# The second half of a key stack read behind the shift rows

## The reference

```python
x = x + tanh(g_xattn) * xattn(layernorm(x), ctx)
x = x + tanh(g_ffn)   * ffn(layernorm(x))

def xattn(x, xa):                 # 16 heads of width 8
    q, k, v    = split_heads(x  @ Wqkv     + bqkv)
    qa, ka, va = split_heads(xa @ Wqkv_aux + bqkv_aux)
    p  = softmax(q @ k.T  / sqrt(8))      # the token's own keys
    pa = softmax(q @ ka.T / sqrt(8))      # the context's keys
    return (p @ v * (1 - gate) + pa @ va * gate) @ Wo + bo

def ffn(x):                       # 64 experts of width 64, 8 chosen per token, one shared
    w = top-8 weights within the 4 best of 8 groups of sigmoid(x @ gate_w.T)
    return sum_e w[:, e] * (silu(x @ Wg[e]) * (x @ Wu[e])) @ Wd[e] + shared(x)
```

## Time and profile before

| | |
|---|---|
| three runs | 865.65, 865.96, 867.04 us; median 865.96 |
| profiled execution | 866.37 us, span 864.3 us |
| mean granted TensorE clock | 0.986 of full speed |
| busy: TensorE (matmuls) | 832.1 us, 96% of the span |
| TensorE (weight loads) | 647.3 us, 75% |
| DVE | 692.8 us, 80% |
| POOL | 635.6 us, 74% |
| ACT | 570.1 us, 66% |
| SP's and ACT's DMA queue | 57.6% and 0.5% of 16 DMA engines' span |
| chain that ended last | PE 85%, DVE 5%, DMA 3%, issue 3%, ACT 2% |

### The profile page before, as it was taken

The page is one execution under the profiler, slowest core; times in us unless marked ns, Lnnn a source line. Parts: engine busy times, 40 slices in busy tenths (PEclk is TensorE's granted clock), DMA queues, the critical chain, the costliest instruction groups (busy, mean ns, idle before and its releaser), DMA issues.

```text
span 864.3 us, 20204 instructions
## 1 busy us (share of the span) xinstructions
PE 832.1 (96%) x6733; PEld 647.3 (75%) x6733; DVE 692.8 (80%) x1656; ACT 570.1 (66%) x964; POOL 635.6 (74%) x602
## 2 busy tenths in 40 slices
PE   4899999999999889999999999999999999999997
PEld 2467777777766678888888888878888888888885
DVE  6788888888888769769788887867886977886655
ACT  4378888888877766575566666558557556656554
POOL 2567888888864368777886887677787788788785
PEclk9599999999999999999999999999999999999999
DMA  4668777787663156556555654754755655655552
GB/s 118 164 157 175 168 180 162 165 183 156 157 144 68 39 144 155 131 132 148 134 128 143 151 130 114 166 140 103 167 129 133 150 141 124 150 124 151 135 135 61
DMA packets 108035, 120.02 MB, mean 139 GB/s; under 512 B 28560, under 2 KB 70352, under 8 KB 106496
## 3 DMA queue, kind: packets, MB, share of 16 engines
q1 hardware_dynamic: 105056, 118.23, 57.6%
q10 hardware_dynamic: 2880, 0.59, 0.5%
HBM read 103.55 MB, written 14.71 MB: 137 GB/s over the span
## 4 chain that ended last, share of the span: by engine, by line
PE 85%; DVE 5%; DMA 3%; issue 3%; ACT 2%; POOL 0%; SPq 0%; DVEq 0%; ACTq 0%; POOLq 0%
PE bank L1957 20%; PE bank L1958 20%; PE bank L1959 20%; PE bank L1302 6%; PE bank L1289 4%; PE bank L1276 4%; PE bank L1258 2%; DMA stack_q<-nmaxT 2%; PE bank L1246 1%; DVE mx L981 1%; PE bank L1323 1%; DMA cwb<-wts_scratch 1%; PE bank L1252 1%; PE bank L1310 1%; PE bank L1934 1%
## 5 line engine op out<-in xcount | busy, mean ns | idle before, releaser
L1634 POOL TENSOR_TENSOR hid<-act,cwb 128x512 f32<-128x512 f32 x264 | 422.3, 1611 | 128.1 <-DVE act L1861 62.2
L1687 ACT ACTIVATE silu<-bank 128x512 f32<-128x512 f32 x256 | 152.8, 597 | 182.2 <-PE bank L1959 176.9
L1861 DVE TENSOR_TENSOR act<-silu,bank 128x512 f32<-128x512 f32 (+1 forms) x264 | 180.2, 683 | 110.4 <-ACT silu L1687 75.7
L1869 DVE TENSOR_TENSOR hlo<-hid,hhi 128x512 fp32r<-128x512 f32 x256 | 206.8, 808 | 9.9 <-ACT hhi L1693 9.6
L1957 PE MATMUL bank<-xhi,weights_hi 128*128 128x512 f32 x520 | 206.6, 397 | 0.9 <-ACT silu L1687 0.9
L1959 PE MATMUL bank<-xlo,weights_hi 128*128 128x512 f32 x520 | 204.1, 393 | 0.0
L1958 PE MATMUL bank<-xhi,weights_lo 128*128 128x512 f32 x520 | 204.0, 392 | 0.0
L981 DVE TENSOR_REDUCE mx<-bank 128x4 f32<-128x512 f32 x256 | 166.3, 682 | 22.5 <-PE bank L1276 22.1
L1693 ACT ACTIVATE hhi<-hid 128x512 fp32r<-128x512 f32 (+1 forms) x264 | 164.9, 625 | 23.3 <-POOL hid L1634 20.7
L783 ACT ACTIVATE prob<-bank 128x1024 f32<-128x1024 f32 x128 | 131.2, 1025 | 52.0 <-PE bank L1289 48.6
L1957 PEld LDWEIGHTS bank<-xhi,weights_hi 128*128 128x128 f32 x520 | 97.6, 188 | 22.5 <-ACT silu L1687 1.5
(11 more groups left out here) (235 smaller groups left out, 1001.0 us busy)
## 6 DMA issues: line engine op xcount, KB each, us to landing
cwb<-wts_scratch SPq DMA_DIRECT2D x174, 384.0 KB, 5.4
stack_k<-k_scratch SPq DMA_DIRECT2D x30, 256.0 KB, 4.7
k_scratch<-parts_k SPq DMA_DIRECT2D x15, 384.0 KB, 3.2
stack_q<-q_scratch SPq DMA_DIRECT2D x30, 128.0 KB, 2.9
stack_k<-k_scratch SPq DMA_DIRECT2D x30, 128.0 KB, 5.4
q_scratch<-parts_q SPq DMA_DIRECT2D x15, 192.0 KB, 2.2
xin<-in_x_dram SPq DMA_DIRECT2D x16, 128.0 KB, 2.6
cin<-in_ctx_dram SPq DMA_DIRECT2D x16, 128.0 KB, 2.8
```

Of the source, the lines that this page charges most:

```text
L1634: pool.tensor_tensor(h_buf[k][:], a_buf[k][:], cwb[slot][:, q % GP, :], ALU.mult).then_inc(h_ok, 1)
L1687: act.activation(s_buf[k % RS][:], g_bank[k % 2][:], ACT.Silu).then_inc(s_ok, 1)
L1861: nc.vector.tensor_tensor(a_buf[k % RS][at], s_buf[k % RS][at], u_bank[k % 3][at], ALU.mult).then_inc(a_ok, 1)
L1869: nc.vector.tensor_tensor(hlo[k % RH][:], h_buf[k % RS][:], hhi[k % RH][:].bitcast(F32), ALU.subtract).then_inc(hl_ok, 1)
```

## The change

In every chunk that still has a stack to read (n = 0 to 13), the two DMAs of the key stack's half 1 are issued where they stood; then SyncE waits until the shift rows of batch 2n + 2 have landed, and only then issues the two DMAs of half 0. All that stood behind them, `store_x2(n - 1)` first, stands behind the wait too.

```diff
--- before.py
+++ after.py
@@ -425,12 +425,12 @@
                 load_products(stack_q[s][PARTS_AT[half]:PARTS_AT[half] + ROWS_S].rearrange("p h c t -> p (h c t)"),
                               q_v[n], False, half, HH * TC, stk[half][s])
 
-        def load_stack_k(n):
+        def load_stack_k(n, halves=(1, 0)):
 
             s = n % NST
             wait(sp, st_mm, UNITS * CH * (n - NST + 1))
             wait(sp, k_st[n % 2], 16 * ((n + 1) // 2))
-            for half in (1, 0):
+            for half in halves:
                 load_products(stack_k[s][PARTS_AT[half]:PARTS_AT[half] + ROWS_S].rearrange("p h c a t -> p (h c a t)"),
                               k_v[n], True, half, 2 * HH * TC, stk[half][s])
 
@@ -522,7 +522,9 @@
                 if g < LOOPS - 2:
                     expert_weights(g, j)
                 if not last:
-                    load_stack_k(n + 2)
+                    load_stack_k(n + 2, (1,))
+                    wait(sp, shift, 16 * (CH * n + 3))
+                    load_stack_k(n + 2, (0,))
                 if n > 0:
                     store_x2(n - 1, 1 - j)
                 if last and j == 0:
```

## The result

Over 22 executions of each kernel, the changed kernel's median is 868.57 us (865.40 to 872.97) against 866.00 us (864.29 to 868.55). The ratio is 1.0031, with a 95% interval of 1.0019 to 1.0042: slower by 0.3%, 2.6 us. The fastest executions of the two lie 1.1 us apart, but 7 of the changed kernel's 22 are above 870 us and none of the other's is. So the change adds a loss of varying size. The forecast was 865.2 us and no difference.

What follows compares the result with a forecast made beforehand. In attention, matmuls were taken as the bound, with visible loss only in two shift-row stalls. Terms -0.89 + 0.1 = -0.8 us took the 865.96 us median to 865.2, no difference that can be told; 8-in-10 range 864.3 to 868.0.

Steps and rivals of the forecast that it cites:

- The gain: Attention stage: shift rows land in 4.4 us against a budget of 6.3, so TensorE's two stalls go: -0.89 us.
- rival A: Shift rows wait for what is ahead, not the second half; stalls stay, 866.0 up to 867.8 us; chance 0.20.
- The term for the second half: Fifth unit's scores: delayed second half lands at 9.5 us against a 10.4 us budget; 0.1 us put in for edge pairs.
- Rival B: Second half becomes the bound at the even batch's fifth-unit scores, 14 chunks: 869 to 873 us; chance 0.14.
- (4): SyncE's work queued behind the new wait (reads, residual's store, q store) is covered by its wait for POOL: cost 0.
- SyncE's wait of 46.5 us: SyncE's 13 waits for POOL's q split over the attention stage, the cover for the hold, would fall under 15 us.
- All pairs take 16.0 us: Attention stage: with shift rows gone from TensorE's waits, every pair of batches takes 16.0 us.

Runs made afterwards that it cites:

- experiment 9: The changed kernel run once more, unaltered, on the chip of three other runs: 867.13 us, ratio 1.0017 to the kernel before; its profiled execution took 874.32 us.
- Experiment 2: Changed kernel, but all four key reads go out as before the change and only then SyncE waits for the shift rows: 865.99 us, ratio 1.0007.
- Experiment 5: Changed kernel with the hold ended by ACT's third exponential of the odd batch, about 4.0 us after the shift rows' issue, instead of their landing: 865.60 us, 0.9993.
- experiments 10 and 11: Changed kernel with SyncE's hold ended by POOL's q split, 4.47 or 5.16 us after the shift rows' issue: 865.71 us (1.0003) and 870.72 us (1.0075).
- experiment 3: Changed kernel without SyncE's new wait; ACT issues the second half's reads after its third exponential in the odd batch: 867.07 us, ratio 1.0018.
- experiment 12: Changed kernel with q reads behind the key store and the hold ended by ACT's third exponential instead of the rows' landing: 869.48 us, 1.0047.
- experiments 6 and 8: Changed kernel with the hold ended by ACT's fourth exponential: 881.46 us (1.0173); changed kernel with q reads issued behind the key store: 870.31 us (1.0041).
- experiment 13: Changed kernel with the two expert-weight reads moved behind the first half and ahead of the wait for the shift rows: 875.58 us, ratio 1.0118.

## Why the prediction was wrong

**The gain was right.** The rows' landing without the second half beside it was taken as 4.4 us (3.9 to 4.9); it measured 4.0 on average, and both stalls of the earlier trace rows went. That speaks against rival A's outcome: with the second half out of the way the longest landing in the changed profile was 5.4 us, not 6.9, though experiment 9 has one of 6.45 and a wait of 0.4 us behind it. Of rival A's mechanism more is left. Experiment 2, with both halves beside the rows, has a mean of 5.1 us, so holding one of them took off 1.1 us and four fifths stayed. By the rule of the Trainium skill, DMA: Bandwidth & Descriptors, section Queues, rings and completion order, that the prediction set against it (turns between queues, packet by packet), most of the landing should have stayed, and on the mean it did. The longest fell from 6.7 to 5.4 us in the first trace, and that was enough for the stalls. What else is under way counts too: in the chunk of stack 14, with no expert weights read and the first half issued 0.8 us behind s, the rows had landed at 2.1 us.

**The term for the second half was right, at its middle.** Its landing stayed inside the budget of 10.4 us: no 48-row load waited for it in either trace of the changed kernel. Rival B was the right sign for a wrong reason. It named L1276 waiting for the key stack, and that row did come, but for the other half.

**The step that failed is (4), "Cost: 0."** It went as far as the next thing on SyncE, and three of its numbers were short:

- "SyncE is through at s + 4.4 + 1.2 + 0.45 = 166.2, 0.15 us past it" used the mean of the landing. The place was right (the q store went out at s + 6.3 on the mean), but the landing ranged from 2.1 to 5.4 us, to 6.45 in experiment 9. What SyncE has to do by s + 5.92 lets a hold be 4.2 us at most without delay; 5 of 14 holds were 4.6 or more. A long issue (1.6 us) among those behind the hold has the same effect, and no longer falls into a wait.
- It left out the landing of the q store itself. The two held reads, 384 KB, and the store of x2 are now issued just ahead of it, and it takes 3.5 us instead of 2.2. (With the store of x2 alone ahead of it, in experiment 2, it took 2.5.) The 1.3 us more was in no sum, though the same text counted with reads holding up a transfer on ACT's queue.
- "The next first half might go out 0.5 us late, and it has about 2 us" is the step that turned. In the chunk shown above it went out 2.8 us later, nearly all of it by the delays of the q store (1.15 us) and of the reads of q behind it (1.65). The wait of the key store for POOL (9.0 us), which was to take a delay up, fell to 2.1 us in one chunk, and was soon used up. The slack was about right; 2.8 passes it. Its working was not: 167.09 is a load that had already stalled for 0.64 us, and without that 1.35 us is left. The traces give it better: first halves issued up to s + 0.8 were in time in the changed kernel's trace and those from s + 1.05 on were late, and before the change the one in the table of issues above went out 0.8 us ahead of its s. That makes 1.6 to 1.9 us.

Experiment 5 shows that the second point alone fits in the slack, experiments 10 and 11 where the slack ends, and experiment 9 that the late first halves are nearly the whole loss of a bad execution. In experiment 2 the block alone cost nothing that can be told. Experiment 5 differs from the changed kernel only in what ends the hold, at the same mean. What turns a mean that is free (4.0) into 0.3% is then the spread, the holds past about 4.5 us and the long issues behind a hold; that this is so in the executions without a trace is concluded from the curve and two traces, not seen in each.

"SyncE's wait of 46.5 us … falls under 15 us" held (5.6). The wait for the rows was 31.9 us instead of 60, since SyncE itself came later to the wait. "All pairs take 16.0 us" failed in four.

**Open.** The price of late reads without a block (experiment 3, 0.18%) may be the same loop by way of the q store (2.6 us) or ACT's part. How the loss in an execution divides between more stalls and the half-clock stretch behind the longer ones isn't known beyond the two shown. No version was measurably faster than the kernel before: the best (0.9993, 0.9996, 0.9997) have 1 in their intervals, as fits a gain of 0.89 us at most.

## What to carry to other kernels

A wait put into a queue that issues in order has to be costed once around the loop: the landing of the next store beside the transfers it was bunched with, then each wait for that landing, up to the next chunk's first need. Cost it at the late end of what it waits for, not at the mean; where its end is a DMA's landing, hold until an engine's event at a known time instead, and find the edge by moving that event.

## What the runs showed of the hardware

- Behind some stalls of TensorE the granted clock fell to half. After the matmuls had waited 1.8 us (experiment 3) and 2.8 us (experiment 9) it was 0.50 for 3.4 us (the windows above), which added up to 1.7 us. The length of the wait doesn't decide it: behind one of 1.5 us in experiment 12 the clock was 0.52 in the next 2 us (169.50 to 171.50), and behind waits of 1.8 us in experiments 6 and 8 it stayed at 1.00 (175.80 to 182.00 and 56.20 to 62.20). Behind the wait of 1.1 us in the changed kernel's profile it stayed at 1.00 too, as the window from 182.34 above shows.
- A store of 192 KB landed in a median of 2.2 us before the change, 2.5 with a store of 128 KB issued just ahead of it (experiment 2), 3.5 with two reads of 384 KB as well (the changed kernel), and 5.5 with the expert weights in that bunch too (experiment 13), with the same bytes moved in each pair.
- A DMA of 16 KB on another queue (the shift rows) landed 2.1 to 5.4 us after its issue in the changed kernel's profile, with one late landing of 6.45 us in experiment 9. With both halves of a key stack under way on the other queue it took 3.9 to 6.7 us (experiment 2), and 6.9 us in the stalled pair before.
